# Graph layer with residual norm on one core: stages reordered, the final scatter last, dense pairs beneath all stages

## The reference

```python
def _egnn_conv(x, src, dst, edge_attr, W_msg, W_edge, W_root, b):
    msg = x[src] @ W_msg + edge_attr @ W_edge
    agg = jax.ops.segment_max(msg, dst, num_segments=x.shape[0])
    agg = jnp.where(jnp.isneginf(agg), 0.0, agg)
    return agg + x @ W_root + b

c1 = leaky_relu(_egnn_conv(X, src, dst, edge_attr, W1_msg, W1_edge, W1_root, b1))
c2 = leaky_relu(_egnn_conv(c1, src, dst, edge_attr, W2_msg, W2_edge, W2_root, b2))
return _layernorm(x + c2)          # mean and variance of each row, eps 1e-5
```

## Time and profile before

| | |
|---|---|
| median of 3 runs | 1418.65 us (1417.38 to 1426.86) |
| span of the profiled execution, its own time | 1697.5 us |
| busy in it: PE, DVE, ACT, POOL | 978.8, 1044.2, 666.9, 1055.8 us |
| mean granted TensorE clock | 0.746 of 2.4 GHz |
| first gather of stage one | 11.75 us |
| stage two, first to last scatter | 765.9 to 1072.8 us |
| stage three from | 1079.1 us |
| bytes moved by DMA | 245.87 MB |

### The profile page before, as it was taken

One profiled execution on the slowest core, in us unless ns is written; L12 is line 12 of the kernel. 1 busy time (PEld: TensorE's weight loads), 2 busy tenths in 40 slices (PEclk: granted clock), 3 DMA queues, 4 the chain that ended last, 5 costly groups with the idle time before them and its releaser, 6 DMA issues.

```text
span 1697.5 us, 21367 instructions
## 1 busy us (share of the span) xinstructions
PE 978.8 (58%) x3038; PEld 438.7 (26%) x3038; DVE 1044.2 (62%) x3881; ACT 666.9 (39%) x1717; POOL 1055.8 (62%) x1182
## 2 busy tenths in 40 slices
PE   3476866666666465687778778454343443334441
PEld 1233433233333232332322223222111111111210
DVE  2356666555555465679999999665544555445553
ACT  1345654444444354568888888400000000000000
POOL 5566656455545545617877767666667766677665
PEclk9678877778777777889999999755655655556555
DMA  6366756556555455755444444533333333233320
GB/s 172 93 183 207 240 178 181 174 175 194 175 177 184 146 179 171 220 177 185 157 153 154 152 146 154 164 111 106 104 95 94 107 99 104 79 102 99 107 74 21
DMA packets 142053, 245.87 MB, mean 145 GB/s; under 512 B 31470, under 2 KB 70120, under 8 KB 142022
## 3 DMA queue, kind: packets, MB, share of 16 engines
q1 hardware_dynamic: 103462, 161.26, 30.4%
q0 software_dynamic: 31360, 45.90, 11.5%
q10 hardware_dynamic: 7200, 38.40, 6.0%
HBM read 122.70 MB, written 125.07 MB: 146 GB/s over the span
## 4 chain that ended last, share of the span: by engine, by line
issue 34%; DVE 15%; PE 15%; another core or an unknown queue 15%; ACT 11%; POOL 4%; DMA 1%; DVEq 1%; ACTq 1%; POOLq 1%
ACT ob L686 5%; PE ps L529 5%; PE ps_r L529 4%; DVE stat L820 3%; PE ps_t L519 2%; POOL out L302 2%; PE ps_m L529 2%; DVE c1t L780 2%; DVE mv L831 2%; ACT c2t L647 2%; POOL g_src L295 2%; DVE c2t L780 2%; DVE stage L923 1%; DVE mx L790 1%
## 5 line engine op out<-in xcount | busy, mean ns | idle before, releaser
L686 ACT ACTIVATE ob<-ps_y,shift,rstd 128x96 f32<-128x96 f32 x784 | 273.7, 432 | 139.9 <-DVE shift L859 71.4
L820 DVE BATCH_NORM_STATS2 stat<-ps_y 128x6 f32<-128x96 f32 x784 | 147.0, 248 | 192.4 <-remote 141.1
L302 POOL DMA_INDIRECT agg_table<-stage,now_end x196 | 221.2, 1128 | 68.5 <-issue 68.2
L302 POOL DMA_INDIRECT out<-stage,now_end x196 | 200.4, 1022 | 60.0 <-issue 59.1
L295 POOL DMA_INDIRECT g_src<-in_x,now_gat x196 | 195.8, 999 | 63.0 <-issue 62.9
L295 POOL DMA_INDIRECT g_dst<-in_x,now_gat x196 | 195.2, 996 | 59.7 <-issue 59.1
L529 PE MATMUL ps<-xtb,wr 97*96 97x512 f32 x392 | 224.1, 655 | 11.0 <-ACT c1t L647 2.9
L295 POOL DMA_INDIRECT g_src<-agg_table,now_gat x196 | 196.8, 1004 | 52.9 <-issue 52.6
L529 PE MATMUL ps<-c1t,wr 97*96 97x512 f32 x392 | 212.4, 625 | 11.5 <-issue 10.3
L519 PE MATMUL ps_t<-ident,g_src 128*96 128x128 f32 x392 | 90.2, 374 | 209.9 <-DMA g_src<-agg_table,now_gat 176.7
L655 ACT ACTIVATE std<-mv,epsc 128x4 f32<-128x4 f32 x245 | 74.6, 305 | 296.5 <-issue 185.5
(11 more groups left out here) (54 smaller groups left out, 1494.3 us busy)
## 6 DMA issues: line engine op xcount, KB each, us to landing
xtb<-in_xt SPq DMA_DIRECT2D x196, 192.0 KB
agg_table<-zero ACTq DMA_DIRECT2D x50, 750.0 KB
out<-ob SPq DMA_DIRECT2D x195, 192.0 KB
mask<-mask_row SPq DMA_DIRECT2D x98, 192.0 KB
xd_keep<-g_dst SPq DMA_DIRECT2D x49, 192.0 KB
root_keep<-rt SPq DMA_DIRECT2D x49, 192.0 KB
c1d_keep<-c1d SPq DMA_DIRECT2D x49, 192.0 KB
rt<-root_keep SPq DMA_DIRECT2D x49, 192.0 KB
```

What stands on the lines that cost most here:

```text
L302: nc.gpsimd.indirect_dma_start(out=rows, out_offset=bass.IndirectOffsetOnAxis(ap=now_end[:, e.slot(R), r:r + 1], axis=0), in_=stage[:, e.s ...
L686: last = nc.scalar.activation(ob[:, d.slot(R), row(r)], ps_y[k][:, row(r)], ACT.Identity, bias=shift[:, k, r:r + 1], scale=rstd[:, k, r:r ...
L820: last = V.bn_stats(stat[:, k, r, :], rows(r))
```

## The change

The program is written anew with the same chunks. The stages are now: one, source rows alone, with 6 dense pairs beneath; two, the scatter to the table, with 35 pairs; three, the second layer, with 33 pairs; and four, the scatter to `out`, with the last 24 pairs beneath it. A pair is 1024 rows (J = 8 rows of x per partition), 98 in all. All loops are written out. The norm works in row form: the second product writes rows (ps_z), the residual comes from x loaded as rows (xn), and one bn_stats serves two rows. The own rows x[dst] are gathered for ten chunks in stage one and for the others in stage three; the first layer at dst is computed in stage three from them and `nat`, so c1d_keep and xd_keep are gone. `nat` is overwritten with the normalised edge rows and scattered from there. Rows that don't end a group go to a place of their own behind the table or `out` (end_i from `aside`), without a bounds check. Every scatter waits for its rows and for the landing of the scatter eight back, on one of eight semaphores. g_src has six buffers, g_dst ten. In stage four a chunk waits for the stored pairs that it overwrites, by a count that a register load reads from pair_i.

```diff
-XR = 2 * R
-PEEL = 2
+J = 8
+HJ = J // 2
+RS = 6
+RD = 10
+NA = 6
+NS = 35
+NM = 33
+AHEAD = 4
+LAND = 8
+CLEARS = 40
+def spread(count, ticks, first):
+    return {t: range(first + t * count // ticks, first + (t + 1) * count // ticks) for t in range(ticks)}
...
+            def gather(rows, index, c, where, k, landed):
+                for r in range(TPC):
+                    t = c * TPC + r
+                    nc.gpsimd.indirect_dma_start(
+                        out=where[:, k, row(r)], out_offset=None, in_=rows,
+                        in_offset=bass.IndirectOffsetOnAxis(ap=index[:, t:t + 1], axis=0),
+                    ).then_inc(landed[k], 16)
+
+            def scatter(rows, c, landed, rows_done):
+                for r in range(TPC):
+                    t = c * TPC + r
+                    pool.wait_ge(rows_done, c + 1)
+                    if t >= LAND:
+                        pool.wait_ge(landed[t % LAND], 16 * (t // LAND))
+                    nc.gpsimd.indirect_dma_start(
+                        out=rows, out_offset=bass.IndirectOffsetOnAxis(ap=end_i[:, t:t + 1], axis=0),
+                        in_=nat[:, t, :], in_offset=None).then_inc(landed[t % LAND], 16)
+
+            pool.wait_ge(s_src, 16)
+
+            for c in range(NCH):
+                if c >= RS:
+                    pool.wait_ge(a_t, c - RS + 1)
+                gather(x, src_i, c, g_src, c % RS, l_src)
+                if c in EARLY:
+                    pool.wait_ge(s_prep, 10)
+                    gather(x, own_i, EARLY[c], g_dst, EARLY[c], l_dst)
+
+            pool.wait_ge(s_cleared, 16 * NZ)
+            for c in range(NCH):
+                scatter(table, c, sc_t, a_nc)
+            for k in range(LAND):
+                pool.wait_ge(sc_t[k], 16 * ((NT + LAND - 1 - k) // LAND))
+
+            for c in range(NCH):
+                e = NCH + c
+                if c >= RS:
+                    pool.wait_ge(b_t, c - RS + 1)
+                else:
+                    pool.wait_ge(a_t, e - RS + 1)
+                gather(table[0:N, :], src_i, c, g_src, e % RS, l_src)
+                o = c + AHEAD
+                if RD <= o < NCH:
+                    pool.wait_ge(e_y, o - RD + 1)
+                    gather(x, own_i, o, g_dst, o % RD, l_dst)
+
+            for c in range(NCH):
+                last = (c + 1) * TPC - 1
+                pool.wait_ge(s_stored, nc.gpsimd.value_load(pair_i[P - 1:P, last:last + 1], min_val=1, max_val=NQ))
+                pool.sem_inc(s_under, 1)
+                pool.wait_ge(s_under, c + 1)
+                scatter(out, c, sc_o, e_done)
+            for k in range(LAND):
+                pool.wait_ge(sc_o[k], 16 * ((NT + LAND - 1 - k) // LAND))
...
+            def layer2(q, h):
+                if not real(q):
+                    return
+                pe.wait_ge(d_c1, 2 * q + h + 1)
+                if q >= 1:
+                    pe.wait_ge(d_u, 2 * (q - 1) + h + 1)
+                for j in range(HJ):
+                    last = nc.tensor.matmul(ps_z[:, h, row(j)], c1t[:, q % 2, cols(h * HJ + j)], wr2[:, :],
+                                            start=True, stop=True)
+                last.then_inc(d_2, 1)
+
+            def dense(steps, h):
+                for d in steps:
+                    layer2(d - 1, h)
+                    layer1(d, h)
...
+            def sums_back(c):
+                pe.wait_ge(b_c1d, c + 1)
+                pe.wait_ge(b_scan, c + 1)
+                if c >= 1:
+                    pe.wait_ge(e_u, c)
+                else:
+                    pe.wait_ge(a_nc, NCH)
+                for r in range(TPC):
+                    nc.tensor.matmul(ps_n[:, row(r)], c1d[:, c % 2, cols(r)], wr2[:, :], start=True, stop=False)
+                    last = nc.tensor.matmul(ps_n[:, row(r)], mx2[:, c % 2, cols(r)], ident[0:D, 0:D],
+                                            start=False, stop=True)
+                last.then_inc(b_n, 1)
...
+                if c < NCH:
+                    pe.wait_ge(l_dst[c % RD], 64 * (c // RD) + 64)
+                    pe.wait_ge(b_z1, c + 1)
+                    forward(g_dst[:, c % RD, :], b_own)
+                    dense(STEPS_B[c], 1)
+                    pe.wait_ge(b_c1, c + 1)
+                    pe.wait_ge(l_ea[k], 16 * (e // R) + 16)
+                    if c >= 1:
+                        pe.wait_ge(b_scan, c)
+                    else:
+                        pe.wait_ge(a_scan, NCH)
+                    product(ps_m, wm2[:, :], xe[:, k, :], b_m)
+                    pe.wait_ge(b_xd, c + 1)
+                    if c >= 1:
+                        pe.wait_ge(b_c1d, c)
+                    else:
+                        pe.wait_ge(a_rc, NCH)
+                    nc.tensor.matmul(ps_r[0:D, :], wr1[0:D, :], xd[:, c % 2, :], start=True, stop=False)
+                    for r in range(TPC):
+                        last = nc.tensor.matmul(ps_r[0:D, cols(r)], nat[:, c * TPC + r, :], ident[:, :],
+                                                start=False, stop=r == TPC - 1)
+                    last.then_inc(b_r, 1)
...
+            def dense_y(q):
+                if not real(q):
+                    return
+                dve.wait_ge(d_u, 2 * q + 2)
+                t = yo[:, q % YR, :]
+                V.tensor_tensor(t, t, xn[:, q % XR, :], ALU.add).then_inc(d_y, 1)
+
+            def dense_stats(q):
+                if not real(q):
+                    return
+                dve.wait_ge(d_y, q + 1)
+                if q >= 2:
+                    dve.wait_ge(d_std, q - 1)
+                    dve.wait_ge(d_shift, q - 1)
+                    dve.wait_ge(d_done_v, q - 1)
+                for j in range(0, J, 2):
+                    last = V.bn_stats(stat[:, q % 2, j:j + 2, :].rearrange("p r s -> p (r s)"),
+                                      two_rows(yo[:, q % YR, j * D:(j + 2) * D]))
+                last.then_inc(d_stats, 1)
```

More of the change, by code:

```diff
@@ L485, in _ @@
             for k in range(R):
[L486 to L487 removed]
+                sp.wait_ge(k_rt[k], 16 * ((NCH + R - 1 - k) // R))
             sp.wait_ge(a_r, NCH)
[L489 to L496 removed]
@@ L498, in store_last @@
[L498 to L507 removed]
+            sp.wait_ge(a_scan, NCH)
@@ L510, in _ @@
+            load_back(0)
+            load_back(1)
+            for t in range(NCH):
+                load_back(t + 2)
+                dense(STEPS_B[t])
+            dense(range(LATE, NQ + 3))
+            stored(NQ - 1)
+            for k in range(YR):
+                sp.wait_ge(o_st[k], 16 * ((NQ + YR - 1 - k) // YR))
         @block.tensor
@@ L566, in step_a @@
[L566 to L582 removed]
+                k = q % XR
@@ L637, in _ @@
+            for d in range(LATE + 1, NQ + 1):
+                for h in range(2):
+                    dense(range(d, d + 1), h)
         @block.scalar
@@ L728, in _ @@
-            clear(NZ - 1)
-            each_chunk(act, step_a)
-            maxima(LAST_CHUNK)
-            def step_s(q, s, last=False):
-                c = chunk(q, s)
-                act.wait_ge(a_nc, c.at + 1)
-                if c.reached(2):
-                    act.wait_ge(sc[c.slot(2)], 64 * c.turn(2))
-                copy(stage[:, c.slot(2), :], nat[:, ds(c.at * TPC * D, TPC * D)], s_stage)
-                for t in range(2):
-                    dense(block_s(q, s, t))
-            each_chunk(act, step_s)
@@ L742, in _, with dense_t1 @@
-            for d in DRAIN:
-                dense(d)
-            def sums(c):
-                if c.reached(0):
-                    act.wait_ge(b_n, c.at + 1)
-                    if c.reached(2):
-                        act.wait_ge(ln[EDGE]["done"], c.before(1).at)
-                    copy(yn[:, c.slot(2), :], ps_n[:, 0:TPC * D], b_nc)
-                    norm_std(EDGE, c)
-            each_chunk(act, lambda q, s, last=False: sums(chunk(q, s).before(1)))
-            sums(LAST_CHUNK)
+            def dense_t1(q, h):
+                if not real(q):
+                    return
+                act.wait_ge(d_1, 2 * q + h + 1)
+                if q >= 2:
+                    act.wait_ge(d_2, 2 * (q - 2) + h + 1)
+                nc.scalar.activation(c1t[0:D, q % 2, half(h)], ps_1[0:D, h, :],
+                                     ACT.Copy, scale=SLOPE).then_inc(d_t1, 1)
@@ L755, in _ @@
+            for d in range(LATE + 2, NQ + 2):
+                dense_head(range(d, d + 1))
+                dense_tail(range(d, d + 1))
             act.wait_ge(s_cleared, 16 * NZ)
```

1071 lines of the change are left out of this document (462 added, 609 removed).

## The result

| | |
|---|---|
| changed kernel | 1300.7 us median of 4 (1300.02 to 1301.02) |
| kernel before | 1418.02 us median of 4 (1415.9 to 1426.86) |
| ratio | 0.9161, 95% interval 0.913 to 0.9192 |
| profiled execution after | 1300.48 us, span 1298.3 us |

The forecast was 1323 us, the range 1275 to 1395. The kernel is faster, and the sum of the prediction holds to 2%. But the experiments found something that neither the profile before nor my reading of it had told: on three other chips the kernel before takes 1676 to 1711 us, and on the one of them where the changed kernel itself ran it takes 1831 us, *more* than before (ratio 1.1013).

A forecast was written before the change was run, and what follows sets the result against it. POOL's indirect-DMA issue rate was taken to bound the changed kernel: 3.5 + 295 + 263 + 6 + 440 + 265 + 10.8 = 1283 us, plus a 40 us remainder, gives 1323 us; range 1275 to 1395.

The forecast's parts named there:

- POOL's issue rate as the bound: Stages one and three: POOL starts an indirect DMA every 1.25 us; free scatters every 1.28 us.
- Stage one, two and final, start and end: Forecast terms: stage one 295 us, stage two 263, final scatter 265, start 3.5, end 10.8.
- The 10 us of contention in stage two: Stage two: yo + xn, VectorE's one two-SBUF-input operation per pair, adds 10 us to 253 us of free scatters.
- The 8 us for register loads: Final scatter: 49 register loads with waits, priced at 8 us between bounds of 0 and 39.
- The landing wait at 0: Scatters: waiting for the landing eight back costs 0, since eight scatters are 9 us of issue.
- Stage three, 440 forecast: Stage three: 196 source gathers and 156 own ones, 352 x 1.25 = 440 us.
- The remainder of 40 us: Gather stages: of 56 us by which before's median exceeded its summed steps, spread over those stages, 40 us stay.
- An unprofiled run holds at most a sixth of that idle time: Kernel before: of 334 us idle POOL time in the profiled 1697.5 us span, unprofiled runs hold only 56 us.
- rival C: Looped streams: their own cost, if the whole 56 us, goes with straight code, giving 1283 us; chance 0.13.
- A: Stages one and three: the engines' chain sets the pace, 10 us a chunk in three; 1345 to 1400 us; chance 0.25.
- B: Stage three: PE stays at 1.2 GHz, 13.4 us a chunk, 1540 us, slower than before; chance 0.06.
- D: Scatters: register loads (1354 us) or landings of 12 us (125 us more, 1448) stop POOL; chance 0.06.

The follow-up runs named there:

- Experiment 12: Changed kernel with two waited index copies (rests) on POOL before each chunk's scatters and gathers, and an s_prep wait; chip 8: 1472.8 us, 1.0353 of before.
- experiment 8: Changed kernel with three register loads per chunk of the final scatter instead of one; chip 12: 1814.5 us, ratio 1.0571 to before.
- experiment 3: Changed kernel with each scatter waiting for the landing four back instead of eight; chip 14: 1820.4 us, ratio 1.0779 to before.
- experiment 11: Changed kernel with two waited index copies (a rest) on POOL before each chunk's scatters, stage two and final; chip 15: 1554.9 us, ratio 0.9256 to before.
- experiment 10: Changed kernel, paced: stage two scatters a chunk once pairs planned four chunks back are summed; chip 15: 1643.5 us, ratio 0.9869 to before.

## Why the prediction was right, and where not

**POOL's issue rate as the bound: right, on the chips where before takes 1418 us.** 1.25 us per gather in stages one and three, 1.26 per free scatter, and 2.2 us from the end of the last scatter of stage two to stage three (6 forecast). Experiment 12 shows it by adding POOL time.

**Stage one, two and final, start and end:** within 3 us each. Behind these agreements stand misses that cancel. A free scatter starts every 1.263 us, not 1.28, and my 253 in stage two is not even 196 x 1.28, which is 251; measured, 196 of them are 248. The 10 us of contention in stage two were 16. In the final stage the 6 for contention were 18: 22 scatters of about 1.37 us, and seven of 1.6 to 2.35 us, each issued across all or nearly all of yo + xn as in the rows above. The 8 us for register loads were 0 (experiment 8). The landing wait at 0 is right, with room to spare (experiment 3).

**Stage three, 440 forecast, 458 measured:** its 18 us are contention as well, which I had left out there: 33 pairs' and 49 edges' sums, gathers of mostly 1.1 to 1.4 us.

**The remainder of 40 us: the step that was mis-sized.** Measured, all that lies over 1283 is 15 us (span 1298.3), and no remainder is needed for it: contention is 55 us where the sum had 16, and the loads, the border, the scatter's interval, start and end are together 23 us less than their terms. That 40 us stood for these 15 made the forecast too long by 22 us. POOL was busy 986 us for the same reason, where I had looked for about 950. I took the 56 us by which before stood over its sum as something that gather stages have. Of its own causes, the loops cost 35 us on chip 14; on the other kind they were not tried, so rival C (1283) may be right in its mechanism; the time lies between it and the forecast.

**"An unprofiled run holds at most a sixth of that idle time": wrong as a reading.** The 334 us of idle POOL in the span of 1697.5 belong to the chip, not to the profiling: on chips 14, 12 and 15 unprofiled runs take 1654 to 1733 us, and after the change the span and the runs agree. I compared a profile of one kind of chip with times of another. The forecast survived because it was summed from POOL's own steps and left the idle time out, and by luck: the comparison met a chip where before takes 1418 us. On chip 15 the same forecast is 508 us too low, and the kernel is slower where it said faster.

**Rivals.** A (engines pace stages one and three): not in the result, with DMA at 268 GB/s as computed and 0.84 busy. On chip 15 stage three takes 11.5 us a chunk even in experiment 11, beyond A's 10. B (PE at 1.2 GHz in stage three): no, 0.89 of 2.4 GHz; PE fell to 0.52 in stage two and 0.59 in the final one, where a pair then takes 6.7 us (403.25 to 409.97) and not 5.2, and 35 of them are 235 us, still under 263. I had priced VectorE and ScalarE for that stage and left PE out, which is the busiest engine beneath it (237 of 255 us); the cover was thinner than I took it for. D: no, loads and landings are free; its 125 us for landings of 12 us should have been 0.22 x 392 = 86, as 12 us over eight scatters are 1.5 each, not 1.6. None of the rivals was the way in which it does come out slower: on chip 15 an unbroken run of indirect DMAs delays what PE signals, POOL runs ahead in stage two because nothing there waits for the engines, and pays for it in stage three and in the final stage. The old stage two did not have that run of DMAs: its scatters went 4 per 6.1 us in lockstep.

**Open:** what differs between the chips, why PE's signals come out late, whether POOL's issuing holds them up or the landings of its scatters (both change together in every run), and from which rate on. The number of DMAs alone does not tell: on chip 15, from 400 us on, 38 to 40 in 50 us delay ACT by over 10 us in the mean, and with rests 29 to 33 by nothing; but 29 to 34 go with 0.5 us or less in stage three of the changed kernel, and 33 to 36 with 2 to 8 us in its final stage, where unbroken runs and waits alternate. The changed kernel itself ran on one chip of the slower kind only; on chips 12 and 14 it was its variants. Also open is a kernel best on both kinds. By the stages, rests in the two scatter stages alone would be 1301 + 55 + 47 = 1403 us where before takes 1418 (worked out, not run), and 1555 where it takes 1676; the paced wait should cost nothing on the first (not run, experiment 10).

## What to carry to other kernels

If a profile's span and the timed runs disagree by more than the runs among themselves, ask first whether they come from the same chip, and run both kernels again elsewhere before a gain is believed. Where a queue of one engine carries the kernel, sum its instructions one by one; keep VectorE sums of two SBUF tiles away from GpSimd's indirect DMAs. And let the engine that issues them feel the others: a wait that the trace of one chip shows always satisfied was worth 188 us on another.

## What the runs showed of the hardware

- Two kinds of chip: before 1418 to 1421 us (result, chip 8) and 1676 to 1711 (chips 12, 14, 15), with equal durations of single instructions (medians on both: free scatter 0.96 us, yo + xn 0.94, copy of c1t 0.58).
- On the second kind, TensorE's completions reach ScalarE and VectorE 26 us late in the rows shown, and up to 67, while POOL issues indirect DMAs 1.26 us apart, and its recorded semaphore updates are then at least 5.6 us apart; completions of ScalarE and VectorE reach TensorE in 0.05 to 0.14 us at the same time.
- A VectorE sum with two SBUF inputs makes an indirect DMA's issue 0.41 us longer in most cases, 0.91 in experiment 11 (1.88 against 0.97), up to 1.4 in the result; the lengthened issue ends 0.83 us after the sum in the median. With one input in PSUM it costs nothing (0.95 us, 64 issues).
- A register load on GpSimd between indirect DMAs costs nothing, three in a row neither.
